# Differential attention at the head of a long kernel: the first batch's rows loaded alone, the other rows, their statistics and later tables inside the stage's own schedule

## The reference

```python
x = x + _L0_attn_a_ref(_layernorm(x), Wq, Wk, Wv, Wproj, lq1, lk1, lq2, lk2)
# then: mixture of experts, routed attention, mixture of experts,
#       state space, FP4 ffn, full attention, FP4 ffn

def _L0_attn_a_ref(x, Wq, Wk, Wv, Wproj, lq1, lk1, lq2, lk2):      # H = 8 heads, hd = 16
    q = (x @ Wq.T).reshape(B, T, 2 * H, hd)
    k = (x @ Wk.T).reshape(B, T, 2 * H, hd)
    v = (x @ Wv.T).reshape(B, T, H, 2 * hd)
    q = apply_rotary(rmsnorm(q), cos, sin)
    k = apply_rotary(rmsnorm(k), cos, sin)
    scores = einsum("bhqd,bhkd->bhqk", q / sqrt(hd), k), causal mask
    attn = softmax(scores).reshape(B, H, 2, T, T)
    lam = exp(sum(lq1 * lk1)) - exp(sum(lq2 * lk2)) + LAMBDA_INIT
    attn = attn[:, :, 0] - lam * attn[:, :, 1]
    out = layernorm(einsum("bhqk,bhkd->bhqd", attn, v)) * (1 - LAMBDA_INIT)
    return out.transpose(...).reshape(B, T, C) @ Wproj.T
```

## Time and profile before

| what | us |
|---|---|
| median of three runs | 4507.12 |
| the three runs | 4502.03, 4507.12, 4533.18 |
| the profiled execution | 4518.29 |
| its span on the core | 4516.5 |
| first weight load of the attention issued | 24.79 |
| first matmul | 39.09 |

### The profile page before, as it was taken

The page is one execution under the profiler, slowest core; times in us unless marked ns, Lnnn a source line. Parts: engine busy times, 40 slices in busy tenths (PEclk is TensorE's granted clock), DMA queues, the critical chain, the costliest instruction groups (busy, mean ns, idle before and its releaser), DMA issues. The chain is left out here.

```text
span 4516.5 us, 59985 instructions
## 1 busy us (share of the span) xinstructions
PE 3778.8 (84%) x19225; PEld 2609.4 (58%) x19288; DVE 2862.9 (63%) x5340; ACT 1914.0 (42%) x3859; POOL 1565.2 (35%) x1463
## 2 busy tenths in 40 slices
PE   3888879799599999988898588876885888888898
PEld 2555558688488888877787244444663333333566
DVE  6566547556465555546565477877884565654788
ACT  2555544344355555453343444422221455545232
POOL 3556525444466655436443201100002333330000
PEclk8888879899799999999999789897997799987899
DMA  5889821455100000002455100000002444440000
GB/s 138 255 217 279 239 75 58 141 166 158 47 10 11 15 15 11 1 18 73 154 160 157 57 10 19 19 1 14 0 0 52 101 96 83 99 82 15 5 14 19
DMA packets 221650, 348.36 MB, mean 77 GB/s; under 512 B 34632, under 2 KB 126266, under 8 KB 215226
## 3 DMA queue, kind: packets, MB, share of 16 engines
q1 hardware_dynamic: 198714, 260.66, 19.4%
q0 software_dynamic: 22656, 84.24, 8.2%
HBM read 166.29 MB, written 169.87 MB: 74 GB/s over the span
## 5 line engine op out<-in xcount | busy, mean ns | idle before, releaser
L2752 DVE TENSOR_REDUCE ab_nmx<-banks 128x1 f32<-128x512 f32 x512 | 334.8, 685 | 227.6 <-PE banks L2568 226.8
L2694 ACT ACTIVATE ab_pt<-banks 128x512 f32<-128x512 f32 x512 | 273.8, 600 | 97.8 <-PE banks L2578 85.7
L1645 POOL TENSOR_TENSOR lb_pq<-lb_pq,lb_rr 128x512 f32<-128x512 f32 x192 | 203.9, 1066 | 306.8 <-DVE lb_rr L1524 303.8
L2578 PE MATMUL banks<-ab_qT,ab_kT 49*128 49x512 f32 x512 | 236.1, 511 | 57.6 <-ACT ab_pt L2694 51.3
L1399 ACT ACTIVATE lb_pq<-banks,lb_nmx 128x256 f32<-128x256 f32 x384 | 178.9, 471 | 220.3 <-DVE lb_nmx L1519 217.5
L2568 PE MATMUL banks<-ab_kT,ab_qT 48*128 48x512 f32 x512 | 238.8, 513 | 28.8 <-DMA ab_kT<-ab_spill 17.1
L2578 PEld LDWEIGHTS banks<-ab_qT,ab_kT 49*128 49x128 f32 x512 | 94.5, 200 | 279.2 <-ACT ab_pt L2694 157.6
L1519 DVE TENSOR_REDUCE lb_nmx<-banks 128x2 f32<-128x512 f32 x192 | 131.4, 685 | 185.3 <-PE banks L1251 184.3
L615 POOL DMA_INDIRECT mb_xi<-moe_ys,moe_b_place x64 | 64.3, 1004 | 386.9 <-DVE mb_uT L2026 338.8
L347 ACT ACTIVATE da_pt<-banks 128x512 f32<-128x512 f32 (+1 forms) x384 | 175.0, 535 | 22.2 <-PE banks L265 20.1
L2806 POOL DMA_DIRECT2D ab_kT<-in_ab_ones x4 | 2.1, 545 | 524.7 <-POOLq L2958 524.7
(11 more groups left out here) (559 smaller groups left out, 11476.9 us busy)
## 6 DMA issues: line engine op xcount, KB each, us to landing
moe_xs<-zero SPq DMA_DIRECT2D x71, 512.0 KB, 11.0
moe_ys<-zero SPq DMA_DIRECT2D x71, 512.0 KB, 10.9
moe_a_w_raw<-in_moe_w SPq DMA_DIRECT2D x48, 512.0 KB, 3.7
moe_b_w_raw<-in_moe_w SPq DMA_DIRECT2D x48, 512.0 KB, 3.7
da_spill<-da_hi SPq DMA_DIRECT2D x128, 128.0 KB, 2.4
ab_spill<-ab_hi SPq DMA_DIRECT2D x128, 128.0 KB, 2.4
da_qT<-da_spill POOLq DMA_DIRECT2D x32, 384.0 KB, 7.0
da_kT<-da_spill POOLq DMA_DIRECT2D x32, 384.0 KB, 9.8
```

Source lines behind the costliest of these rows:

```text
L1645: nc.gpsimd.tensor_tensor(pq[:, n % RING, :, :], pq[:, n % RING, :, :], bcast(rr[:, n % RING, :], 2, 2 * P), ALU.mult).then_inc(s_p, 1)
L2578: nc.tensor.matmul(ps[:, EXP_BANK + n % 3, :], kT[b % 2][r:r + AB_ROWS + 1, p, j * P:(j + 1) * P], qT[b % 2][r:r + AB_ROWS + 1, p, :], sta ...
L2694: nc.scalar.activation(pt[:, s % RING, :], ps[:, EXP_BANK + s % 3, :], ACT.Exp, scale=AB_D ** -0.5).then_inc(s_e, 1)
L2752: nc.vector.tensor_reduce(nmx[:, g % 2, col:col + 1], ps[:, MAX_BANK + n % 3, :], op=ALU.max, axis=AX.X, negate=True).then_inc(s_mx, 1)
```

## The change

The first block loads only the first batch's rows, the identity and the attention's tables; VectorE sets its constants there and nothing else. diff_attention gets the semaphores of the rows and two functions. load_rows issues the rows of batches 1 to 7 on SP, right behind the two weight loads. load_tables issues the "moe" and "lb" tables on SP after the spills of batch 0, where beside stands for the later batches. The statistics, the root and the reciprocal are now done for each batch: "stats" at slot -39 of the batch on DVE, "row" at -37 on ACT, and the reciprocal (with a drain) at the head of normal, at -33. For batch 0 these three stand ahead of the loop; for batch b they fall at -23, -21 and -17 of batch b - 1. In the opening ACT does lambda's exponential and the first root ahead of the casts of the weights, and DVE does the statistics, lambda's sums, the constants in vx and the normalising of batch 0 ahead of the weights' low halves.

```diff
@@ -140,7 +140,7 @@
     return done
 
 
-def diff_attention(core, w, a, spill, beside):
+def diff_attention(core, w, a, spill, beside, s_x, load_rows, load_tables):
 
 
 
@@ -157,11 +157,11 @@
              (-16, "v", 0), (-15, "v", 1), (-14, "turn", 0), (-13, "turn", 1), (-12, "turn", 2), (-11, "turn", 3),
              (29, "heads", 0), (29, "heads", 1), (31, "out", 0), (32, "out", 1)]
     table += [(2 * hv + 5, "back", hv) for hv in range(DA_H)]
-    vector_table = [(-33, "normal", 0), (-28, "xlo", 0), (-25, "sum", 0), (-24, "sum", 1), (-23, "sum", 2), (-22, "sum", 3),
+    vector_table = [(-39, "stats", 0), (-33, "normal", 0), (-28, "xlo", 0), (-25, "sum", 0), (-24, "sum", 1), (-23, "sum", 2), (-22, "sum", 3),
                     (-20, "rms", 0), (-20, "scaled", 0), (-20, "scaled", 1), (-19, "scaled", 2), (-19, "scaled", 3),
                     (-18, "rope", 0), (-18, "rope", 1), (-17, "rope", 2), (-17, "rope", 3),
                     (20, "mean", 0), (21, "centre", 0), (22, "square", 0), (23, "var", 0), (27, "scale", 0)]
-    scalar_table = [(-21, "rms", 0), (27, "std", 0)]
+    scalar_table = [(-37, "row", 0), (-21, "rms", 0), (27, "std", 0)]
     pool_table = [(-29, "xhi", 0), (-26, "square", 0), (-25, "square", 1), (-24, "square", 2), (-23, "square", 3),
                   (-19, "swap", 0), (-19, "swap", 1), (-18, "swap", 2), (-17, "swap", 3),
                   (-9, "stack", 0), (-9, "stack", 1), (-1, "stack", 2), (-1, "stack", 3)]
@@ -210,7 +210,7 @@
         outT = core.xnT
         lams, nlam, lprod = sb("lams", [P, 4]), sb("nlam", [P, 1]), sb("lprod", [P, 2, DA_D])
 
-        s_std, s_lam, s_ready, s_w, s_whi = (sem(x) for x in ("std", "lam", "ready", "w", "whi"))
+        s_mv, s_std, s_lam, s_ready, s_w, s_whi = (sem(x) for x in ("mv", "std", "lam", "ready", "w", "whi"))
         s_xn, s_raw, s_xhi, s_xlo, s_qkv, s_v, s_sq, s_sum, s_rms, s_qn, s_swap, s_rope, s_thi, s_hl = (
             sem(x) for x in ("xn", "raw", "xhi", "xlo", "qkv", "v", "sq", "sum", "rms", "qn", "swap", "rope", "thi", "hl"))
         s_s, s_e, s_tri, s_av, s_osb, s_att, s_var, s_std2, s_ln, s_outT = (
@@ -234,6 +234,7 @@
             def _(sp):
                 sp.dma_start(raw_wqk, a["da_wqk"].rearrange("(c p) n -> p c n", p=P)).then_inc(s_w, 16)
                 sp.dma_start(raw_wv, a["da_wv"].rearrange("(c p) n -> p c n", p=P)).then_inc(s_w, 16)
+                load_rows(sp)
                 for b in range(B):
                     for i in range(CHUNKS):
                         n = CHUNKS * b + i
@@ -247,6 +248,8 @@
                                              src[64 * par:64 * par + 64, n % 2, :].bitcast(F32)).then_inc(s_spill[i], 16)
                     if b:
                         beside(sp, b - 1, B - 1)
+                    else:
+                        load_tables(sp)
 
             @block.tensor
             def _(pe):
@@ -390,7 +393,11 @@
                         act.drain().then_inc(free, 1)
 
                 def root(kind, b):
-                    if kind == "rms":
+                    if kind == "row":
+                        act.wait_ge(s_mv, b + 1)
+                        nc.scalar.activation(core.std[:, b, :], core.mv[:, b, :, 1], ACT.Sqrt, bias=core.eps[:, :],
+                                             scale=1.0).then_inc(s_std, 1)
+                    elif kind == "rms":
                         act.wait_ge(s_sum, NT * (b + 1))
                         nc.scalar.activation(ssum[:, :, :], ssum[:, :, :], ACT.Sqrt, bias=core.rms_eps[:, :],
                                              scale=1.0 / DA_D).then_inc(s_rms, 1)
@@ -399,19 +406,20 @@
                         nc.scalar.activation(var[:, :], var[:, :], ACT.Sqrt, bias=core.eps[:, :],
                                              scale=1.0 / 32).then_inc(s_std2, 1)
 
+                act.wait_ge(s_lam, 1)
+                nc.scalar.activation(lams[:, 2:4], lams[:, 0:2], ACT.Exp).then_inc(s_lam, 1)
+                root("row", 0)
                 act.wait_ge(s_w, 32)
                 nc.scalar.copy(wqk[0][:, :, :], raw_wqk).then_inc(s_whi, 1)
                 nc.scalar.copy(wv[0][:, :, :], raw_wv).then_inc(s_whi, 1)
-                std_of_tokens(core, act, s_std)
-                act.wait_ge(s_lam, 1)
-                nc.scalar.activation(lams[:, 2:4], lams[:, 0:2], ACT.Exp).then_inc(s_lam, 1)
                 for s in range(first_slot, last_slot):
                     for job in odd.get(s - 1, ()):
                         empty(job)
                     if s >= 3 and (s - 3) % 2 == 0 and (s - 3) // 2 < B * DA_H:
                         heads_out((s - 3) // 2)
                     for kind, b, i in scalar_jobs.get(s, ()):
-                        root(kind, b)
+                        if kind != "row" or b:
+                            root(kind, b)
                     if 0 <= s + 2 < NS:
                         exponentials(s + 2)
 
@@ -451,7 +459,15 @@
                             dve.drain()
                             token_stats(core, dve, b)
 
+                def row_stats(b, i):
+                    dve.wait_ge(s_x[b], 16)
+                    token_stats(core, dve, b)
+                    dve.drain().then_inc(s_mv, 1)
+
                 def normal(b, i):
+                    dve.wait_ge(s_std, b + 1)
+                    nc.vector.reciprocal(core.rstd[:, b, :], core.std[:, b, :])
+                    dve.drain()
                     if b:
                         filled(dve, ("x", b - 1, 1))
                     normalise(core, dve, b, s_xn)
@@ -515,15 +531,17 @@
                     dve.drain()
                     nc.vector.tensor_tensor(heads_of(b), heads_of(b), bcast(mean[:, :], 2, 32), ALU.mult).then_inc(s_ln, 1)
 
-                jobs_of = {"normal": normal, "xlo": low_x, "sum": sum_squares, "rms": rms, "scaled": scaled, "rope": rope,
+                jobs_of = {"stats": row_stats, "normal": normal, "xlo": low_x, "sum": sum_squares, "rms": rms, "scaled": scaled, "rope": rope,
                            "mean": mean_of, "centre": centre, "square": square, "var": variance, "scale": rescale}
+                row_stats(0, 0)
+                dve.wait_ge(core.loaded["da"], core.loads["da"] + 16)
+                nc.vector.tensor_tensor(lprod[:, :, :], w["da_lq"][:, :, :], w["da_lk"][:, :, :], ALU.mult)
+                dve.drain()
+                nc.vector.reduce_sum(lams[:, 0:2], lprod[:, :, :], axis=AX.X).then_inc(s_lam, 1)
                 for x in vx:
                     nc.vector.memset(x[:, :, :, 32:33], 1.0)
                     nc.vector.memset(x[:, :, :, 33:64], 0.0)
-                nc.vector.tensor_tensor(lprod[:, :, :], w["da_lq"][:, :, :], w["da_lk"][:, :, :], ALU.mult)
-                dve.drain()
-                nc.vector.reduce_sum(lams[:, 0:2], lprod[:, :, :], axis=AX.X).then_inc(s_lam, 1)
-                rstd_of_tokens(core, dve, s_std)
+                normal(0, 0)
                 dve.wait_ge(s_whi, 2)
                 nc.vector.tensor_tensor(wqk[1][:, :, :], raw_wqk, wqk[0][:, :, :].bitcast(F32), ALU.subtract)
                 nc.vector.tensor_tensor(wv[1][:, :, :], raw_wv, wv[0][:, :, :].bitcast(F32), ALU.subtract)
@@ -536,7 +554,8 @@
                     for job in odd.get(s - 1, ()):
                         empty(job)
                     for kind, b, i in vector_jobs.get(s, ()):
-                        jobs_of[kind](b, i)
+                        if b or kind not in ("stats", "normal"):
+                            jobs_of[kind](b, i)
 
             @block.gpsimd
             def _(pool):
@@ -2928,12 +2947,9 @@
             @block.sync
             def _(sp):
                 with nc.allow_non_contiguous_dma(reason="small tables"):
-                    for b in range(B):
-                        sp.dma_start(core.res[:, b, :, :], x_v[:, b, :, :]).then_inc(s_x[b], 16)
+                    sp.dma_start(core.res[:, 0, :, :], x_v[:, 0, :, :]).then_inc(s_x[0], 16)
                     sp.dma_start(core.ident[:, :], a["ident"]).then_inc(core.loaded["da"], 16)
                     issue(sp, da)
-                    issue(sp, moe_small)
-                    issue(sp, lb)
 
             @block.vector
             def _(dve):
@@ -2941,11 +2957,15 @@
                 nc.vector.memset(core.eps[:, :], LN_EPS)
                 nc.vector.memset(core.rms_eps[:, :], RMS_EPS)
                 nc.vector.memset(core.one[:, :], 1.0)
-                for b in range(B):
-                    dve.wait_ge(s_x[b], 16)
-                    token_stats(core, dve, b)
-                    dve.drain()
-                dve.wait_ge(core.loaded["da"], core.loads["da"] + 16)
+
+        def load_rows(sp):
+            for b in range(1, B):
+                sp.dma_start(core.res[:, b, :, :], x_v[:, b, :, :]).then_inc(s_x[b], 16)
+
+        def load_tables(sp):
+            with nc.allow_non_contiguous_dma(reason="small tables"):
+                issue(sp, moe_small)
+                issue(sp, lb)
 
```

(3 more changed lines are left out.)

## The result

| | us |
|---|---|
| kernel before, median of 6 runs (4490.43 to 4533.18) | 4506.24 |
| changed kernel, median of 6 runs (4470.18 to 4494.79) | 4481.15 |
| ratio of the two | 0.9942, 95% interval 0.9921 to 0.9963 |
| forecast (range) | 4486 (4473 to 4503) |

The gain is 4506.24 - 4481.15 = 25 us (17 to 36 by the interval). A repetition of the unedited changed kernel gave a ratio of 0.9955 (0.9935 to 0.9975), that is 20 us, and medians 28 us apart (8 runs with a median of 4485.67, and 4513.61 for the kernel before). The forecast was 21.

What follows compares the result with a forecast made beforehand. The first stage was taken as mostly TensorE's own work, its opening bound by SyncE's issuing, a DMA landing and vector and scalar work. 23.8 - 1.1 - 1.5 - 0 = 21.2 us gained gave 4486 us, range 4473 to 4503.

Steps and rivals of the forecast that it cites:

- The first block gets short: Opening, SyncE: 8 DMAs issued in place of 35, 0.55 us each, so the attention block starts at 5.5 us.
- Weights landed: Opening: both attention weight loads, issued at 5.5 and 5.95 us, land at 10.0 to 12.4, taken as 10.8.
- The first transpose: Opening, TensorE: starts at 15.3 us in place of 39.09, a gain of 23.8 us (22.3 to 24.7).
- Statistics, 1.1 us lost in the first preparation: VectorE, between batch 0's third and fourth sum of squares: 2.17 us added against 1.22 idle, losing 1.1 us.
- Hidden in the middle batches: VectorE after the third sum: 2.17 us of statistics a batch fit into idle time, with 3.78 us more slack.
- Roots and reciprocals, 1.5 us: One added root and reciprocal per batch; the reciprocal in VectorE's longest run loses 1.5 us (0 to 2.1).
- Moved DMAs, 0: Residual loads behind the weights, twenty tables behind batch 0's spills: no loss taken, range 0 to 2.5 us.
- rule of turns between queues: DMA engines alternate between queues with work; by it the tables take turns with da_kT, against the forecast of no loss.
- the rival of 7 us: Tables slow da_kT's landing in batch 0 by 7 us, leaving a gain of 14, 4493 us; chance 0.15.
- The rival in which the weights wait for the rows behind them: Opening: weights land with the seven residual loads at 19 us, first transpose at 23, total 4494; chance 0.08.
- The sum: Whole kernel: opening gain 23.8 less 1.1 statistics, 1.5 short operations and 0 DMAs gives 21.2 us; forecast chance 0.62.
- the run of work up to the residual add: Rival: statistics push VectorE's longest run, 2.17 us a batch where TensorE waits; gain 6, 4501 us; chance 0.07.

Runs made afterwards that it cites:

- lean: Changed kernel with first rows alone in the first block, weights issued before ident and attention tables, lambda and second batch's statistics later; median 4491.90 us, ratio to before 0.9930.
- stats_x2: Changed kernel with the statistics of batches 1 to 7 computed twice in the same place; first router matmul at 637.8 us, idle time behind first score 80.6.
- stats_x4: Changed kernel with the statistics of batches 1 to 7 computed four times in the same place; 4516.08 us, ratio to before 1.0018.
- b_new_order: Kernel before with only the opening's ScalarE and VectorE work in the changed kernel's order; first transpose at 35.54 us, first score 1.5 us earlier.
- tables_early: Changed kernel with the twenty later tables issued right behind the seven residual loads; first score at 73.48 us, TensorE's wait for da_kT 8.9 us.

## Why the prediction was right

*The first block gets short*: right, but the issues took 0.45 to 0.5 us where I took 0.55, and the weights were issued at 5.03, not 5.5. *Weights landed* at 10.57 (10.8 taken), the tables of the attention 2.8 us after their issue (4.0 taken). The first transpose at 14.37 (15.3 forecast, 14.4 to 16.8 as the range): a gain of 24.7 in place of 23.8. The last link was another one than in the sum. There VectorE's own work ended at 12.9, half a microsecond behind the casts; measured, VectorE was free at 11.4, since the tables had landed early, and the low halves waited 0.74 us for the casts. So the landing of the weights bounds the opening, by less than a microsecond.

*Statistics, 1.1 us lost in the first preparation*: 27.4 - 26.35 = 1.0 from first projection to first turn; the six kernels with one set of statistics in that place have 27.1 to 27.4, the three without and lean, where they were moved away, 26.2 to 26.5. *Hidden in the middle batches*: shown by stats_x2 and stats_x4, with a cover of 4.2 to 4.8 us, somewhat more than the slack of 3.78 us read from the earlier trace rows (3.37 in the changed kernel). I had counted the third batch's statistics among the hidden ones. They stand just ahead of the first exponentials; computed once, they cost little there: TensorE's idle time from the first score to the first value matmul is 0 in both executions of the kernel before, 1.0 us in b_new_order, and 0.4 to 1.1 in six of the seven kernels that have them, with 2.6 in tables_early.

*Roots and reciprocals, 1.5 us*: the idle time behind the first score is 75.8, 75.6 and 77.6 in the three kernels without them (mean 76.3), and 77.3 to 80.6 in the seven kernels with one set of statistics a batch (mean 78.7). That is 2.4 us, somewhat more than my 0 to 2.1, but the spread within each group is 2 to 3 us, and which instruction costs it stays open; part may be statistics that are not quite hidden. Two waits repeat better than the sum: that for the residual add is 25.0 to 25.2 us in the three and 25.7 to 25.9 in the seven, that for the exponentials 31.1 to 31.3 and 32.1 to 32.4. That fits a reciprocal and a root on those paths; it doesn't prove it. With the statistics doubled the first was 24.7 and the second 32.9, so the growth of the first at least is not the statistics'.

*Moved DMAs, 0*: right, by the landing of da_kT with and without the tables (9.8 and 9.9 us in the mean) and by tables_early. The Trainium skill's rule of turns between queues ("DMA: Bandwidth & Descriptors", "Queues, rings and completion order") may well act here, which no run shows; it has no price that these runs can see, and the rival of 7 us is out. The rival in which the weights wait for the rows behind them is out too: they landed at 10.6 while seven residual loads stood behind them. Behind the rows, they waited.

The sum was 21.2; the marks give 24.5 at the first score less 2.4 behind it, 22; two sets of runs gave 25 and 20. Some of the closeness is luck: the 24.5 hold 0.9 us by which the leg from the first turn to the first score was shorter in the changed kernel's profile (25.95 and 26.80), and that leg varies by more from kernel to kernel. The median, 4481, lies 5 us below the forecast. Of that 1 us is the opening's and 1 us the kernel before, whose median of six runs is 4506.2 where three gave 4507.1; the rest is within the spread of single runs, 25 us from the lowest to the highest of the changed kernel and 43 of the one before.

What I had wrong is what would break first if the cover failed: I named the run of work up to the residual add; it was ScalarE's wait for the last sum of squares, with the exponentials behind it.

## What to carry to other kernels

Ask of a kernel's opening what is ahead of the first load that the first matmul hangs on: tables and rows for later were worth 13 and 11 us here, or 21 together, and at their new places they cost nothing that could be seen. The statistics, roots and reciprocals that had to move with the rows cost some 3. Work that moves into a running schedule is free only up to the idle time ahead of the next wait that others queue behind; read that time from the timeline (3.8 us here), for the batches at the edge of the schedule by themselves, and test it by computing the work two and four times over. When the expected gain is half a per cent, compare marks within the stage and idle time, not the spans of two profiles.

## What the runs showed of the hardware

TensorE's pace drifts from execution to execution at an unchanged program. In the full attention of the kernel before, some 2635 matmuls were busy for 558 us at a granted clock of 0.91 in one execution and for 532 at 0.95 in the other. This made one pair of profiles differ by twice the true gain. And a load's landing depends on its neighbours in the queue more than on its size: a residual load of 512 KB took 3.9 us as the first in an empty queue, and the eight had a median of 8.2; the identity, 64 KB, took 3.6 us behind one residual load and 7.7 behind eight.
